# Direct products for the first head group, batch 1 projected in step 0, context keys spread per group, and down products with the rounded half first

## What is computed

```
h = layernorm(x)
q, k, v = heads(h @ Wq + bq), heads(h @ Wk + bk), heads(h @ Wv + bv)
y = softmax(causal(q k^T * scale)) v
qc, kc, vc = heads(h @ Wcq + bcq), heads(ctx @ Wck + bck), heads(ctx @ Wcv + bcv)
y = y + softmax(qc kc^T * scale) vc
x = x + y @ Wp + bp
h = layernorm(x)
aff = sigmoid(h @ Wr + br); w = top8(aff) / (sum(top8(aff)) + 1e-9)
shared = (silu(h @ Wg_s + bg_s) * (h @ Wu_s + bu_s)) @ Wd_s + bd_s
routed = sum_e w[e] * ((silu(h @ Wg[e] + bg[e]) * (h @ Wu[e] + bu[e])) @ Wd[e] + bd[e])
x = x + shared + routed
```

## Time and profile before

| | us |
|---|---|
| median of three runs | 200.59 |
| the profiled execution, its own time | 200.57 |
| its span | 198.8 |
| PE busy in it | 186.6 |
| step 0 begins (scores) | 19.44 |
| step 1 begins | 26.67 |
| last FFN product's end | 194.7 |

### The profile page before, as it was taken

How to read it: one execution, slowest core, us unless ns; L and a number is a source line. 1 busy time by engine, 2 the same in 40 slices (tenths; PEclk the granted TensorE clock), 3 DMA queues, 4 the chain that set the end, 5 groups by cost and what they waited for, 6 DMA issues and landing times.

```text
span 198.8 us, 3994 instructions
## 1 busy us (share of the span) xinstructions
PE 186.6 (94%) x1242; PEld 138.3 (70%) x1254; DVE 149.9 (75%) x343; ACT 137.7 (69%) x280; POOL 111.5 (56%) x181
## 2 busy tenths in 40 slices
PE   7869999999999999998999999896999999999993
PEld 2537667777777777775776886584888888887661
DVE  2999997577569865895692889758577888887982
ACT  3546899787898898987789556945455556555571
POOL 6889994565495799749637485983422333000020
PEclk9999999999999999999999999999999999999999
DMA  4364423232243223501211112120000000000003
GB/s 113 106 146 122 116 74 87 50 80 71 71 113 95 61 73 89 120 2 41 52 34 40 40 25 58 39 62 2 0 0 3 0 0 0 0 2 0 3 0 106
DMA packets 20434, 10.40 MB, mean 52 GB/s; under 512 B 11881, under 2 KB 18542, under 8 KB 20414
## 3 DMA queue, kind: packets, MB, share of 16 engines
q1 hardware_dynamic: 19290, 9.24, 18.5%
q0 software_dynamic: 672, 0.69, 1.4%
q10 hardware_dynamic: 452, 0.23, 0.5%
HBM read 4.51 MB, written 0.52 MB: 25 GB/s over the span
## 4 chain that ended last, share of the span: by engine, by line
PE 73%; POOL 10%; DVE 8%; issue 3%; ACT 2%; DMA 1%; DVEq 0%; ACTq 0%
PE psum L1418 11%; PE psum L1419 10%; PE psum L1420 10%; PE psum L1519 6%; PE psum L1575 5%; PE psum L1612 5%; PE psum L1600 4%; PE psum L1622 4%; PE psum L1580 3%; POOL ckey_rows L457 3%; PE psum L1748 3%; PE psum L1584 2%; PE psum L1518 2%; POOL key_rows L443 2%; PE psum L1541 2%
## 5 line engine op out<-in xcount | busy, mean ns | idle before, releaser
L983 ACT ACTIVATE gate<-psum,bias_cols 128x512 f32<-128x512 f32 (+2 forms) x35 | 23.5, 675 | 26.9 <-PE psum L1420 26.9
L845 ACT ACTIVATE probs<-psum 128x512 f32<-128x512 f32 x64 | 36.3, 596 | 2.3 <-PE psum L1580 1.1
L739 POOL TENSOR_TENSOR hid_lo<-hid,hid_hi 128x512 fp32r<-128x512 f32 x13 | 16.8, 1289 | 32.0 <-ACT hid_hi L992 31.9
L1362 DVE SCALAR_TENSOR_TENSOR gated<-psum,bias_cols,gate 128x512 f32<-128x512 f32 x32 | 23.9, 748 | 11.7 <-ACT gate L983 11.7
L1519 PE MATMUL psum<-key_blocks,query_rows 96*128 96x512 f32 x48 | 24.1, 544 | 1.6 <-DVE key_blocks L1052 1.6
L1374 DVE TENSOR_TENSOR hid<-gated,psum 128x512 f32<-128x512 f32 x32 | 21.9, 684 | 2.1 <-PE psum L1748 0.6
L658 POOL TENSOR_TENSOR w_late_lo<-w_ffn,w_late_hi 128x384 fp32r<-128x384 f32 x11 | 12.7, 1162 | 18.0 <-ACT w_late_hi L857 18.0
L992 ACT CAST hid_hi<-hid 128x512 fp32r<-128x512 f32 (+1 forms) x33 | 20.2, 613 | 1.6 <-DVE hid L1374 1.0
L1146 DVE TENSOR_REDUCE row_max<-psum 128x4 fp32r<-128x512 f32 x16 | 11.0, 688 | 13.4 <-PE psum L1519 13.4
L1150 DVE TENSOR_REDUCE row_max<-psum 128x4 fp32r<-128x1024 f32 x16 | 19.4, 1214 | 0.0
L1418 PE MATMUL psum<-xT_hi,w_late_hi 128*128 128x512 f32 x42 | 16.8, 400 | 0.0
(11 more groups left out here) (208 smaller groups left out, 512.1 us busy)
## 6 DMA issues: line engine op xcount, KB each, us to landing
query_rows<-queries SPq DMA_DIRECT2D x46, 64.0 KB, 2.1
key_rows<-keys SPq DMA_DIRECT2D x39, 32.0 KB, 1.9
w_ffn<-in_L_ffn_Wg SPq DMA_DIRECT2D x16, 64.0 KB, 2.0
w_ffn<-in_L_ffn_Wu SPq DMA_DIRECT2D x16, 64.0 KB, 2.1
w_ffn<-in_L_ffn_Wd SPq DMA_DIRECT2D x16, 64.0 KB, 2.0
ckey_rows<-ckeys POOLq DMA_DIRECT2D x12, 32.0 KB, 2.1
key_rows<-keys POOLq DMA_DIRECT2D x9, 32.0 KB, 2.2
x_sb<-in_x SPq DMA_DIRECT2D x2, 128.0 KB, 2.7
```

What stands on the lines that cost most here:

```text
L845: act.activation(probs[:, i % 2, c, :], bank(B_ST + c % 2), ACT.Exp, scale=SCALE).then_inc(exp_done, 1)
L983: act.activation(gate[rows_of(n), n % 3, part], psum[of, B_GATE + n % 2, part], ACT.Silu, bias=bias_cols[of, BIAS_GATE + u:BIAS_GATE + u + ...
L1362: dve.scalar_tensor_tensor(out=gated[:, n % 3, :], in0=bank(B_UP + n % 2), scalar=bias_cols[:, BIAS_UP + u:BIAS_UP + u + 1], in1=gate[:, n ...
```

## The change

**Direct products.** Group 0 of batch 0 isn't placed by DMA. `w_direct_hi` and `w_direct_lo` hold the 32 columns of the first group three times, so a tripled product with them (`project_direct`, 96 rows) leaves each channel in the three places in PSUM. ACT rounds it into key_rows or query_rows (`round_direct`), DVE overwrites the one third that must be the lower rest (`split_direct`). The rows of every group 0 are then ordered by part and not by channel, and `head_mask` gets a second column set for it.

**Batch 1 and the rest.** Batch 1 is turned, projected and split within step 0; x_pair moves to step 2, "keys_queries" to steps 3 and 5, "cross_values" to steps 4 and 6. Steps 2 and 3 have all four key blocks made by ACT (ACT_ALONE). Tiles 2 and 3 are normalized by ACT instead of DVE, the statistics of tiles 4 to 7 are taken by DVE in step 1, their norm by ACT in step 2. Step 0 has two turns of maxima (`first_turn`) and two shifts (`first_shift`), so that scores(0, 0) need not wait for the context.

**Context keys.** POOL spreads all of them: of batch 0 in one operation for four heads (`first_ctx`), of batches 1 to 3 in four operations a group, one group in each of steps 0 to 3 (`later_ctx`). Who issues which placement changes too.

**Values' biases** (bv, bcv) are no longer added to the values; since the weights of a softmax sum to one, their sum is added to y when y is rounded (`y_bias`).

**FFN.** The down product of an item is the two with `hid_hi`, and then the one with `hid_lo`; the first two wait for `hid_hi` alone. The last item's first two stand ahead of the lower part of the item before. route_turn of batch 2 moves from slot A to B of item 6, that of batch 3 from item 10 to 11. POOL's weight splits move by one item from item 4 on.

```diff
+ACT_ALONE = (2, 3)
...
-        tail_at = {0: [("x_pair", FIRST_BATCHES)]}
-        for b in range(FIRST_BATCHES, BATCH):
-            tail_at[2 * b - 3] = [("keys_queries", b)]
-            tail_at[2 * b - 2] = [("cross_values", b)]
+        tail_at = {0: [("values", 1)], 2: [("x_pair", 2)]}
+        for b in range(2, BATCH):
+            tail_at[2 * b - 1] = [("keys_queries", b)]
+            tail_at[2 * b] = [("cross_values", b)]
...
-                     (6, "A"): [("route_turn", 2)],
+                     (6, "B"): [("route_turn", 2)],
...
-                     (10, "B"): [("route_turn", 3)]}
+                     (LEAD - 1, "B"): [("route_turn", 3)]}
...
+            def spread_ctx(g, batches, done):
+
+                n = batches.stop - batches.start
+                rows = ckey_rows[0:ROWS, g, :].rearrange("p (b k) -> p b k", b=BATCH)[:, batches, :].bitcast(F32)
+                mask = head_mask[0:ROWS, int(g == 0), :]
+                if n == 1:
+                    pool.tensor_tensor(ckey_blocks[0:ROWS, g, 0, :, :], rows.to_broadcast([ROWS, GROUP, CTX]),
+                                       mask.unsqueeze(2).to_broadcast([ROWS, GROUP, CTX]),
+                                       ALU.mult).then_inc(done, 1)
+                    return
+                for j in range(GROUP):
+                    ins = pool.tensor_tensor(ckey_blocks[0:ROWS, g, batches, j, :], rows,
+                                             mask[:, j:j + 1].unsqueeze(2).to_broadcast([ROWS, n, CTX]), ALU.mult)
+                ins.then_inc(done, 1)
...
+                of = n if n >= RSTD_ITEM else n + 1
+                if of in ROUND_AT and n != RSTD_ITEM - 1:
+                    split_unit(ROUND_AT[of])
...
+            def round_direct(k):
+
+                to = (key_rows[0:SHIFT_ROW, 0, 0, :], query_rows[0:SHIFT_ROW, 0, 0, 0, :],
+                      query_rows[0:SHIFT_ROW, 0, 0, 1, :])[k]
+                bias = ORDER[k][1] + BIAS_DIRECT
+                act.wait_ge(m_direct, k + 1)
+                if k == 0:
+                    act.wait_ge(rows_set, 1)
+                act.activation(to, psum[0:SHIFT_ROW, B_DIRECT[k], 0:SEQ], ACT.Identity,
+                               bias=bias_cols[0:SHIFT_ROW, bias:bias + 1]).then_inc(direct_rounded, 1)
...
+            act.wait_ge(have_neg_mean, 1)
+            norm(2)
+            norm(3)
+            round_x(1)
+            first_shift(0)
+            expand(1)
+            exps(0, (0,))
+            act.wait_ge(m_v, 1)
+            act.wait_ge(zeroed, 1)
+            act.copy(value[:, 0:2, :, 0:D],
+                     value_bank(0).rearrange("p (t h d) -> p t h d", t=2, h=HEADS)).then_inc(have_value, 1)
+            first_shift(1)
+            exps(0, (1,))
             expand(2)
-            act.wait_ge(have_neg_mean, 1)
-            norm(4)
-            norm(5)
+            for n in range(3):
+                round_qkc(1, n)
             exps(0, (2, 3))
             shift(1)
...
+                if i == 2:
+                    act.wait_ge(have_neg_mean, 2)
+                    for t in range(4, TILES):
+                        norm(t)
...
                 if i == 0:
-                    pe.wait_ge(qkc_split, 3 * FIRST_BATCHES)
-                scores(i, 0)
-                scores(i, 1)
-                if i == 0:
+                    pe.wait_ge(qkc_split, 3)
+                    project_values(0)
+                    pe.wait_ge(xT_split, 2)
+                    pe.wait_ge(have_ffn_bias, 1)
+                    project_qkc(1, 0)
+                    project_qkc(1, 1)
+                    pe.wait_ge(have_value, 1)
+                    project_qkc(1, 2)
                     natural(1)
-                    context_values()
-                    scores(0, 2)
                     scores(0, 3)
...
                     if m < LAST_ITEM:
+                        pe.wait_ge(hid_rounded, m + 1)
+                        down_part(y, down_hi, hid_hi[rows, m % 3, :])
+                        down_part(y, down_lo, hid_hi[rows, m % 3, :])
+                        if m == LAST_ITEM - 1:
+                            for h, part in enumerate(HALVES):
+                                last = hi_of(SHARED)[INNER:P, 2, :], lo_of(SHARED)[INNER:P, 2, :]
+                                pe.wait_ge(last_hi, h + 1)
+                                for weights in last:
+                                    down_part(y[:, part], weights, hid_hi[INNER:P, LAST_ITEM % 3, part])
                         pe.wait_ge(*lo_done(m))
...
```

More of the change, by code:

```diff
@@ L393, in value_bank @@
         def value_bank(b):
[L395 to L396 removed]
+            half = b > 0
+            return psum[:, B_MISC if half else B_OUT, SEQ * half:SEQ * (half + 1)]
         def turned_bank(i):
@@ new lines, in _ @@
+            act.wait_ge(t_bias, 1)
+            act.copy(bias_cols[:, BIAS_Q:BIAS_ROWS], bank(B_BIAS, 2 * BIAS_DIRECT)).then_inc(have_bias_cols, 1)
+            act.wait_ge(have_bias_cols, 1)
+            act.wait_ge(m_ck, 1)
+            act.activation(ckeys[:, 0, :], bank(B_CK, CTX_KEYS), ACT.Identity,
+                           bias=bias_cols[:, BIAS_CK:BIAS_CK + 1]).then_inc(ck_rounded, 1)
+            round_direct(0)
+            round_direct(1)
+            round_qkc(0, 0)
+            expand(0)
@@ L869, in tail @@
                 if name == "y_turn":
+                    act.wait_ge(have_y_bias, 1)
                     act.wait_ge(t_y, b + 1)
-                    copy_hi(yT_hi[:, :], bank(B_MISC, SEQ), yT_rounded)
+                    act.activation(yT_hi[:, :], bank(B_MISC, SEQ), ACT.Identity,
+                                   bias=y_bias[:, 0:1]).then_inc(yT_rounded, 1)
                 if name == "x2_turn":
@@ L1196, in tail @@
                     split_qkc(b, 1)
+                if name == "values":
+                    values(b)
+                    cvalues()
                 if name == "cross_values":
@@ L1201, in tail @@
                     dve.wait_ge(yT_rounded, b + 1)
-                    lo_half(yT_lo[:, :], bank(B_MISC, SEQ), yT_hi[:, :], yT_split)
+                    dve.wait_ge(have_y_bias, 1)
+                    dve.scalar_tensor_tensor(out=yT_lo[:, :], in0=bank(B_MISC, SEQ), scalar=y_bias[:, 0:1],
+                                             in1=yT_hi[:, :].bitcast(F32), op0=ALU.add,
+                                             op1=ALU.subtract).then_inc(yT_split, 1)
                 if name == "project":
@@ L1630, in tail @@
                 take_misc(reader, 3 * b + 2 if name == "keys_queries" else b + 1)
+                if name == "values":
+                    project_values(b)
+                    context_values()
                 if name == "x_pair":
@@ L1792, in _ @@
                             pe.wait_ge(last_lo, h + 1)
-                            ins = product3(y[:, part], hi_of(u)[rows, 2, :], lo_of(u)[rows, 2, :],
-                                           hid_hi[rows, m % 3, part], hid_lo[rows, m % 3, part], start=False)
+                            ins = down_part(y[:, part], down_hi, hid_lo[rows, m % 3, part], stop=True)
                         ins.then_inc(m_down, 1)
```

530 lines of the change are left out of this document (298 added, 232 removed).

## The result

The changed kernel took **202.64 us** (median of four executions, 202.22 to 202.8), beside 200.69 us for the kernel before on the same chip: a ratio of 1.0088, with a 95% interval of 1.0059 to 1.0116. It is slower, by 1.8 us by the ratio and 1.95 by the medians. The forecast was 199.5 us, faster, with 201.6 as the upper end of its range. Ratios here leave out executions more than 1.5% above the fastest of their kernel; medians leave out none.

What follows compares the result with a forecast made beforehand. PE was taken as full from step 1's scores on, idle only before 26.67 us, in the first twelve FFN items and in the last 5 us. Sum: 200.57 - 1.1 + 2.6 - 1.95 - 0.5 - 0.1 = 199.5 us, range 197.5 to 201.6.

Steps and rivals of the forecast that it cites:

- A: Start of step 1: first key blocks come earlier, ACT's queue eats most of it; scores(1) at 25.6 instead of 26.67, -1.1 us.
- Rival 4: Step 0: PE stands, its clock drops to 1.2 GHz for 5 us of work, adding 2.5 us: 202.0 us; chance 0.05.
- B: Steps 1 to 6: +0.4 turns of x, -0.2 a wait, +0.9 step 2, +1.5 step 6, in sum +2.6 us.
- the collision in the shared bank: Step 6: y_turn waits until batch 3's values are read out of B_MISC, +1.5 us.
- C: First twelve FFN items: waits for routes and lower halves shrink; gate(12) at 139.75 instead of 141.70, -1.95 us.
- rival 2: FFN items: the route wait is moved, not removed, so nothing is won there: 201.5 us; chance 0.17.
- D: The end: four of six products now stand ahead of the wait for the last lower half, -0.5 us.
- Rival 1: Front wins more: ACT's queue overlaps better, -1.9 us at step 1's start, steps 1 to 6 +1.5: 197.6 us; chance 0.18.
- Rival 3: Front and FFN cancel: second var_eps waits out the memset of ckey_rows, 1.0 us, ACT's queue passes it on: 200.5; chance 0.15.
- E: Small gaps of 0.1 before down products: -0.1 us.

Runs made afterwards that it cites:

- run 8: The kernel before with its last five calls of run_idle taken out, nothing else: 204.12 us, ratio 1.0134.
- run 6: run 5 with the turns of x behind step 1's attention and ACT's copy of the turned routes back in slot A of item 6: 199.16 us, 0.9931.
- run 3: The kernel before with the FFN part of the change alone: 198.6 us, ratio 0.9888.
- run 5: The changed kernel with seven more idle products in step 0 and y of batch 0 turned behind the attention of step 5: 200.15 us, ratio 0.9967.
- run 9: run 6 with DVE's ident casts behind the first statistics, the second norms' chain a step earlier and ACT's norms split over steps 1 and 2: 197.92 us, 0.984.
- run 10: The kernel before with the FFN part, but ACT's copy of batch 2's turned routes left in slot A of item 6: 198.09 us, ratio 0.985.
- run 2: The changed kernel with y of batch 0 turned behind the attention of step 5, within step 6: 203.22 us, ratio 0.9988.
- run 1: The changed kernel with seven more idle products on PE ahead of step 1: 202.5 us, ratio 1.0057.
- run 4: The kernel before with only the places of the route turns moved (item 6 slot A to B, item 10 to 11): 199.69 us, ratio 0.9941.

## Why the prediction was wrong

- **A, the start of step 1: right.** -1.0 against -1.1 (my own pieces, 23.25 + 0.5 + 0.6 + 1.1, make 25.45 and not the 25.6 that I wrote; it was 25.65). The second maxima ended at 13.55 (forecast 13.5), natural(1) began at 17.34 (17.1), the second shift ended at 18.46 (18.35), the shift of step 1 at 23.33 (23.25). ACT did set the pace: it was busy 3.15 of 3.20 us from 20.20 on.
- **Rival 4, the clock, was what happened, and is the step that failed.** I wrote that PE would stand more than half the time between 18.7 and 23.3 us (it was busy 2.83 of 4.60, and 1.35 of the last 3.20), called the fall of the clock possible, and gave it 0.05. All four executions have a mean clock of 0.987 to 0.990, and the profiled one shows the fall in step 1. Its price was 1.59 us in step 1, not 2.5: 3.1 us at half rate instead of 5, and 1.1 us net in the time. I had the evidence against my chance in the code: by its code the kernel before issues 33 idle products (run 8 shows that the 21 from 9.9 us on are worth 2.7 us or more to it), the change 24, and no more of them where PE now stands longer. I costed the waits of PE as time and not as what they do to the clock behind them.
- **B, steps 1 to 6.** Step 6 took 7.67 (forecast 7.47), its wait 1.49 (1.5): the collision in the shared bank was right. Step 2 took 6.05, the very number of my term, but that is luck: with the clock up it is 6.38, and its cause was half missed. I had ACT's norms as the only chain; run 6 shows a second one, rstd on POOL to neg_mean on DVE to normalize(0), of which I wrote that it came "no later". Step 1 is where B went wrong, by the clock alone.
- **C, the first items: right in kind, 0.15 to 0.35 too large.** -1.8 alone (run 3), -1.6 in the changed kernel, against -1.95. No wait for routes is left, which rules rival 2 out. What I did not carry through is the wait for the turned routes' copy, 0.69 us: I moved the next turn of x by 0.4 us and took it to be hidden. Nor did the waits for lower halves all vanish: one of 0.42 us is left. PE was idle 1.2 us in the first twelve items, where I had named under 1 as the sign.
- **D, the end: -0.3 (run 3) against -0.5.** I counted two products behind the last lower half; there are three, since the lower half of the item before is finished in the same row of DVE operations. In the changed kernel only 0.1 was left, as 0.3 us were lost between item 12 and the last up products. They belong to the attention part: the changed kernel and all six runs with its attention take 48.01 to 48.04 us over this piece, the kernel before and the five runs with the old attention 47.75 to 47.77. The loss builds up evenly over the piece, without a wait of PE; its cause is open.
- **Outside the terms:** 0.3 us more in step 13, where PE's wait ahead of the attention grew from 0.76 to 1.09 us; and the profiled execution's own time lay 2.0 us above its span, not 1.8.
- **Rivals 1 and 3** did not occur. The front did not win more, since ACT's queue was as full as forecast; the second var_eps took 0.33 us, not 1.0.

In sum, step 7 began 1.9 us later against before than forecast (0.1 from A, 1.6 from the clock in step 1, 0.2 in step 6), step 13 added 0.3, C fell short by 0.35, D and E together by 0.5, and 0.2 came outside the span: 3.3 us, the distance from 199.5 to the 202.8 of the profiled execution, which lies 0.16 above the median.

With 1.1 us less for the clock the time would still have been 201.55 us, slower than before: the clock is the largest single miss, and the sign needed the others too. The FFN part is worth 2.25 us by itself (run 3); the attention part took it back. Up to item 0 that part cost 3.7 us (109.15 against 105.44). Without low clock and without the wait of step 6 (run 5) item 0 began at 106.22, 0.8 late; with the chain of step 2 a step earlier as well (run 9) at 105.14, 0.3 ahead of before. So much is the attention part worth up to there once its waits are mended, and 0.3 us of it is lost again behind item 12. Runs 9 and 10, side by side on one chip, differ by that part, so mended, alone: 197.92 and 198.09 us, ratios of 0.984 and 0.985 with intervals that overlap. What the direct products alone are worth, no run shows.

## What to carry to other kernels

A wait of PE has two prices: its own time (1.85 us in the gaps ahead of step 1), and what the granted clock may make of the next microseconds (here 1.6 us, 1.1 of it net). Where a change opens a gap ahead of full PE work, fill it with idle products or count a stretch at half rate, and look at the clock of every execution and not of the profiled one alone. When two jobs that share a bank are moved into one step, the first reader's whole path on the other engines becomes a wait of PE; the cure here was other PE work between them. And a wait on an engine that is itself paced by PE does not absorb what PE gains.

## What the runs showed of the hardware that I had not expected

- PE gaps of 0.63 and 1.23 us, with 1.35 us of work about them in 3.20 us, were followed by some 3 us at 1.2 GHz, with a mean clock to match in each of four executions; in run 2, the same program up to step 6, in ten of twelve, and in its profile for 6.7 us. With seven idle products there (2.83 of 3.20 us busy) that stretch was gone, and with step 6's gap closed too no execution of eight had one.
- The same single gap of 1.48 us in step 6 was followed by such a stretch in the profiled execution of run 1, and by none in that of the changed kernel, whose gap there was 1.49. Ahead of natural(0) a gap of 1.59 us in run 4 was followed by one, the same gap of 1.55 us in the profile of the kernel before by none. So a kernel with such a gap has two times, about 1.1 us apart, and one profile shows one of them.
- Once low, the clock stayed low for about 19 us in the profiled execution of run 8, although PE was 94% busy for the last 13.5 of them; by the mean clock three of that kernel's six executions had far less of it.
- Over 48 us of full PE work in the FFN, kernels with the changed attention part took 0.26 us more, in seven traces against six, with no wait of PE and the clock at 1.00.
